# A two-layer block on eight cores: second-layer chunks one step later, and the front of the next token tile behind the statistics

## The reference

```
xn   = layernorm(x) * gamma + beta
v, g1, g2 = split(xn @ W_in + b_in)            # 1024 -> 3 x 1024
y    = conv(conv(v, k0) * g1, k1) * g2         # causal, 128 taps, per channel
x    = layernorm(x + (x + y @ W_out + b_out))
# feed-forward with quantized activations and ternary weights
bitlinear(x, nw, w) = quant(rmsnorm(x) * nw) @ ternary(w).T   # quant: round(x * 127 / max|x|) / scale
h    = act_scale * relu(bitlinear(x, norm1_w, w1))**2 + act_bias   # 1024 -> 4096
out  = layernorm(x + bitlinear(h, norm2_w, w2))                    # 4096 -> 1024
```

## Time and profile before

| | us |
|---|---|
| median of 3 runs | 3107.97 (3107.31 to 3112.25) |
| the profiled execution | 3111.75 |
| its span, slowest core (core 4) | 3110.2 |
| spans of the 8 cores | 3085.6 to 3110.2 |
| busy: TensorE / weight load / VectorE / ScalarE / GpSimd | 1383.4 / 430.3 / 1522.5 / 786.9 / 72.7 |
| DMA queue of SyncE (q1) | 186716 packets, 82.34 MB |

### The profile page before, as it was taken

The page is one execution under the profiler, slowest core; times in us unless marked ns, Lnnn a source line. Parts: engine busy times, 40 slices in busy tenths (PEclk is TensorE's granted clock), DMA queues, the critical chain, the costliest instruction groups (busy, mean ns, idle before and its releaser), DMA issues.

```text
span 3110.2 us, 19372 instructions; the slowest of 8 cores (3085.6 to 3110.2 us)
## 1 busy us (share of the span) xinstructions
PE 1383.4 (44%) x4270; PEld 430.3 (14%) x4270; DVE 1522.5 (49%) x1611; ACT 786.9 (25%) x1164; POOL 72.7 (2%) x128
## 2 busy tenths in 40 slices
PE   0666566676666610000023554444554443455453
PEld 0122122222212100000001111111111111111110
DVE  2223434334343434555124566655566665566665
ACT  0010111111111000000004444444444444444442
POOL 0000000000000011101000000000000000000000
PEclk9888777777877755555556666666766666676775
DMA  3410000000000035668830100100110010011011
GB/s 87 142 34 0 11 21 11 11 21 11 21 11 14 7 124 174 208 253 277 195 73 13 27 17 24 24 24 23 26 28 16 23 24 24 23 27 28 15 23 27
DMA packets 203436, 166.43 MB, mean 54 GB/s; under 512 B 173625, under 2 KB 178490, under 8 KB 199227
## 3 DMA queue, kind: packets, MB, share of 16 engines
q1 hardware_dynamic: 186716, 82.34, 10.4%
q0 software_dynamic: 16608, 82.85, 8.5%
HBM read 100.09 MB, written 29.36 MB: 42 GB/s over the span
## 4 chain that ended last, share of the span: by engine, by line
DVE 35%; issue 14%; PEldq 13%; DMA 13%; SPq 9%; ACT 9%; PEld 4%; DVEq 2%; ACTq 1%; POOLq 0%
PEldq L175 13%; DVE g2s L882 8%; DMA wqf<-w 8%; SPq L1014 6%; DVE Pb L656 5%; ACT d2s L875 2%; DVE xq2o L888 2%; DVE f2s L872 2%; DMA xq2Tc<-xq2o 2%; DMA xp<-sc_xp 2%; SPq L837 1%; DVE wqb L804 1%; DVE d2s L885 1%; DVE st_mu L510 1%; SPq L830 1%
## 5 line engine op out<-in xcount | busy, mean ns | idle before, releaser
L1023 PE MATMUL yc<-wq2T,xq2Tc 128*128 128x512 bf16 x1024 | 380.7, 492 | 678.7 <-DMA xq2Tc<-xq2o 666.1
L882 DVE SCALAR_TENSOR_TENSOR g2s<-d2s,g2s 128x1024 bf16<-128x1024 bf16 x288 | 352.9, 1225 | 35.2 <-issue 1.3
L984 PE MATMUL pj<-wq1T,xq1T 128*128 128x512 bf16 x1024 | 305.2, 433 | 120.6 <-DMA xq1T<-xq 84.3
L1023 PEld LDWEIGHTS yc<-wq2T,xq2Tc 128*128 128x128 bf16 x1024 | 110.5, 112 | 941.9 <-issue 911.4
L934 ACT ACTIVATE t<-xp 128x1024 f32<-128x1024 bf16 x16 | 16.9, 1056 | 554.2 <-PEq L175 481.8
L1043 DVE TENSOR_TENSOR t2f<-t2f,nw2r 128x1024 f32<-128x1024 f32 x64 | 78.4, 1225 | 148.8 <-ACTq L175 141.4
L875 ACT ACTIVATE d2s<-f2s 128x1024 bf16<-128x1024 bf16 x64 | 67.6, 1056 | 321.1 <-DVEq L175 321.1
L984 PEld LDWEIGHTS pj<-wq1T,xq1T 128*128 128x128 bf16 x1024 | 99.4, 105 | 334.1 <-issue 270.9
L598 PE MATMUL pj<-Wg,xnT 128*128 128x512 bf16 x288 | 110.6, 553 | 73.1 <-DVEq L175 73.1
L598 PE MATMUL yc<-Wg,xnT 128*128 128x512 bf16 x576 | 136.7, 380 | 2.9
L665 PE MATMUL pj<-Pb,s_winv 128*128 128x512 bf16 x198 | 98.4, 566 | 84.6 <-DVEq L175 84.6
(11 more groups left out here) (181 smaller groups left out, 2054.6 us busy)
## 6 DMA issues: line engine op xcount, KB each, us to landing
wqf<-w POOLq DMA_DIRECT2D x64, 512.0 KB, 4.3
wqf<-w POOLq DMA_DIRECT2D x16, 2048.0 KB, 12.0
wf<-W_in SPq DMA_DIRECT2D x8, 1536.0 KB, 7.1
xr<-x_own POOLq DMA_DIRECT2D x16, 512.0 KB, 4.0
sc_wq<-wqb SPq DMA_DIRECT2D x32, 256.0 KB, 2.4
sc_wq<-wqb SPq DMA_DIRECT2D x8, 1024.0 KB, 5.2
xq2Tc<-xq2o SPq DMA_TRANSPOSE x512, 2.3
out<-outb SPq DMA_DIRECT2D x16, 512.0 KB, 2.9
```

Source lines behind the costliest of these rows:

```text
L882: tn = sch.op("vector", (lambda lv: lambda e: e.scalar_tensor_tensor(gbuf[:, 0:width], dbuf[:, 0:width], 0.5 + lv, gbuf[:, 0:width], OP.is ...
L984: (lambda ss, dc, h: lambda e: e.matmul(pshalf("pj", h), xq1T[:, dc * 128:(dc + 1) * 128], wq1T[dc][:, ss * 1024 + h * 512: ss * 1024 + (h ...
L1023: (lambda k, q, oc, kb: lambda e: e.matmul(pshalf("yc1", oc), xq2Tc[kb][:, q * 128:(q + 1) * 128], wq2Tc[k * 8 + q][:, oc * 512:(oc + 1) * ...
```

## The change

Two things are reordered in stage 3, and nothing else changes.

First, the loop over `k` in a pass runs six steps instead of five, and T chunk `k-2` is emitted in step `k` where it was T chunk `k-1`. The SV chunks and superstrips keep their steps.

Second, F of tile `t+1` is emitted after the statistics of tile `t`, where it stood at the start of the pass; the eight transposes of `xq1` belong to it again and are no longer a function of their own. F is thus followed by the final add of tile `t-1`.

```diff
@@ emit_stageF
         free["t1"] = tq1
-        d["tq1"] = tq1
-        return d
-
-    def emit_xq1T(d):
-        tq1 = d["tq1"]
         trq1 = []
         for c in range(8):
             trq1.append(sch.op("sync", (lambda c: lambda e: e.dma_start(
...
         free["xq1"] = tuple(trq1)
+        return d
@@ the loop over t
         if t == 0:
             Fst[0] = emit_stageF(0)
-            emit_xq1T(Fst[0])
-        if t + 1 < NT:
-            Fst[t + 1] = emit_stageF(t + 1)
         tok_sc = [None] * 4
         tq2s = {}
         tmm2_last = None
-        for k in range(5):
+        for k in range(6):
             if t >= 1 and k < 4:
                 tq2s[k] = emit_chunkSV(t - 1, k)
             if t < NT and 1 <= k <= 4:
                 th2_tok = emit_superstrip(t, k - 1)
                 tok_sc[k - 1] = emit_stat_chunk(t, k - 1, th2_tok)
-            if t >= 1 and k >= 1:
-                tmm2_last = emit_chunkT(t - 1, k - 1, tq2s[k - 1])
-        if t + 1 < NT:
-            emit_xq1T(Fst[t + 1])
+            if t >= 1 and k >= 2:
+                tmm2_last = emit_chunkT(t - 1, k - 2, tq2s[k - 2])
         if t < NT:
             Sst[t] = emit_stats(t, tok_sc)
+        if t + 1 < NT:
+            Fst[t + 1] = emit_stageF(t + 1)
```

## The result

The changed kernel takes 3022.5 us (median of 8 runs, 3020.4 to 3023.6); the kernel before 3108.4 in the same comparison. The ratio is 0.9721 with a 95% interval of 0.9711 to 0.9732: 2.8% faster, 85.9 us. Forecast were 3029.2 and a range of 3011 to 3060. The profiled execution's span is 3021.8 us on core 5 (3110.2 on core 4 before).

A forecast was written before the change was run, and what follows sets the result against it. No engine is full; the stage is a chain with holes, VectorE standing in it most often. 13 x 5.87 = 76.3, + 11.9 - 11.8 + 2.4 = 78.8 us off 3111.75: 3033.0, on the median 3029.2; range 3011 to 3060.

The forecast's parts named there:

- F: Front stage of a tile (L938 to L888 on xq1), forecast to take 14.37 us.
- E3: Moment VectorE ends a tile's fourth SV chunk; E3 to SV0 forecast at 37.37 us against 43.24.
- SV0: First L872 on f2s of the next pass, forecast 8.03 us behind the end of F.
- The wait before stat 3: VectorE's hole before stat 3: superstrip 3 behind T chunk 1 brings it to E3 + 3.9 to 5.6, from 11.6.
- stat 3: The fourth L1043 of a tile on VectorE, forecast at E3 + 3.9 to 5.6.
- The load as the new last wait: Load of xp on SyncE behind T chunk 3's transposes: issued E3 + 10.60, 4.37 us later F starts, E3 + 14.97.
- The tail: After F: final add, sums, normalization, then SV0, 8.03 us with 3.19 idle for the cast F used to cover.
- The ends: First and last tiles of the stage: gain 11.9 us at the start, loss 11.8 at tile 13, gain 2.4 at tile 14.
- stat 3 stays late: Rival: superstrip 3 meets another wait, F starts at E3 + 18.8, 50 us of gain go: 3079; chance 0.06.
- the load takes all the gain: Rival: load of xp reaches VectorE 10.2 us after issue, E3 to SV0 stays 43.2: 3108; chance 0.02.
- superstrip 0 becomes the bound: Rival: next tile's F, transposes and matmuls in series delay Relu 0; slower, 3138 if 31 us; chance 0.04.
- the fourth rival: Transposes issued so fast VectorE never waits for the load; F at about E3 + 11: 2973; chance 0.04.

The follow-up runs named there:

- Experiment 7: Changed kernel with the load of xp ahead of T chunk 0, SV0's cast ahead of the final normalization, and two superstrip accumulators: 2906.8 us, ratio 0.9350.
- Experiment 5: Changed kernel with the load of xp for the next tile issued ahead of T chunk 0, not behind T chunk 3: 2983.7 us, ratio 0.9597.
- experiment 6: Changed kernel with the load of xp ahead of T chunk 0 and the next SV0's cast ahead of the final normalization: 2934.8 us, ratio 0.9436.
- experiment 2: Changed kernel with T chunks back at k-1 in five steps, F still behind the statistics: 3068.0 us, ratio 0.9872 to the kernel before.
- experiment 4: Changed kernel with the eight transposes of xq1 put behind the store of out on SyncE: 3022.5 us, ratio 0.9733 to the kernel before.

## Why the prediction was right, point by point

**In short.** Each wait went and came where the prediction has it, and the median was 6.7 us under the forecast. That the gain a tile came out so close is partly luck: both terms of the difference were too long, and the errors partly cancel. From E3 to SV0 the tile of the earlier trace rows takes 43.24 us, but the thirteen tiles of before take 42.6 on average; afterwards it is 36.3 where 37.37 was forecast. So 0.6 us too much before and 1.1 us too much after left 5.87 forecast against 6.3. Outside E3 to SV0 a tile changed by 0.1 us, which makes up the measured 6.45.

**The wait before stat 3.** Right in its cause. The prediction put stat 3 at E3 + 3.9 to 5.6. It came at 4.7 to 6.1, on average at 5.3; at 5.78 in the tile above, because superstrip 3 ran slow:

```profile
2410.68 6.19 PE L980 MATMUL pj<-wq1T,xq1T 128*128 128x512 bf16 x16 [6.24 <-ACTq L175]
2417.09 3.61 PE L1019 MATMUL yc<-wq2T,xq2Tc 128*128 128x512 bf16 x16 [0.23 <-issue]
```

After 6.24 us of idleness its sixteen matmuls took 6.19 us, at a mean granted clock of 0.60 (1 is full speed, 2.4 GHz; the lower level is 0.5, 1.2 GHz); those of T chunk 2 right behind it took 3.61, at 1.00. So superstrip 3 ran mostly at the lower level after the pause, and the clock was back at the upper one by T chunk 2. The slow value of the earlier trace rows, 6.07, has a clock of 0.61, and the 4.41 one of 0.87; the slower one was nearer. It cost nothing here, since the load was later still. Experiment 7 shows what it is worth once the load is out of the way.

**The load as the new last wait.** Right. F was forecast at E3 + 14.97 and came at 14.82 (14.6 on average): issue 0.17 later than forecast, load to F 4.05 where the earlier trace rows have 4.37. Experiment 5 shows it as the bound. The Trainium skill (Advanced Engine Details and Errata, section X-Bar Transpose (TRN2)) says that transposing DMAs are as fast as regular ones on this chip. The trace does not bear that out for transposes of 32 KB: eight held SyncE for 10.48 us here too, and one load of 256 KB for 0.52. Experiment 5, which moves the load ahead of all 32 transposes of the T chunks, is worth 39 us.

**The tail.** The wait of 3.13 before SV0 is the cast, as forecast (3.19); experiment 6 took it away.

**The mis-sized term: F.** It was given 14.37 us, from one tile, and takes 13.71. Part of this was a choice of row: in that tile VectorE had one stall of 0.54 us before L885, 0.35 above the usual. The other 0.38 was not foreseen. (In most tiles of before F takes 14.0 us, not 14.37.) ScalarE's cast in F, first before and then after:

```profile
2515.60 0.20 ACT L912 ACTIVATE st_tmpb<-st_tmpb 128x1 f32<-128x1 f32 x1
2516.59 1.15 ACT L869 ACTIVATE it2s<-t,st_m 128x1024 int32<-128x1024 f32 x1 [0.79 <-DVEq L175]
```

```profile
2434.63 0.20 ACT L912 ACTIVATE st_tmpb<-st_tmpb 128x1 f32<-128x1 f32 x1
2435.24 1.15 ACT L869 ACTIVATE it2s<-t,st_m 128x1024 int32<-128x1024 f32 x1 [0.41 <-DVEq L175]
```

With the new order the cast waits for one semaphore instead of eight: by the time F comes, ScalarE has already waited for later values of the seven DMA lanes. F's share of the 1.1 us that the forecast had too much in each tile is 0.66; the other 0.4 is F's earlier start. The stretch from SV0 to E3, which the prediction left alone, takes 48.8 us, and took 48.9 before.

**The ends.** Tile 0's SV0 was forecast at 1689.9 and came at 1686.43. Half of that is the superstrips of tile 0, which follow each other in 5.25 us each, where the earlier trace rows have one of 6.96; the rest is F's start (0.65), F itself (0.35) and stat 0 (0.7). In the forecast's own terms the spans give 15.35 us at the start (11.9 forecast), 83.2 in thirteen tiles (76.3), a loss of 10.95 at tile 13 (11.8), 1.4 at tile 14 (75.09 to 73.71, where 2.4 was forecast) and a loss of 0.6 behind it (nothing): 88.4, where 78.8 were forecast. The median moved by 2.5 us less than the span of the profiled executions, whose slowest cores are not the same.

**The rivals.** That stat 3 stays late is what experiment 2 is, and it cost 46 us against the changed kernel, where 50 were worked out for it. That the load takes all the gain, and that superstrip 0 becomes the bound, were tested in experiments 5 and 4 and don't hold. More gain was there to be had by moving the load; no run made the transposes faster, which is what the fourth rival was about, and SyncE's rows speak against it.

## What to carry to other kernels

When no engine is full, follow one tile from a fixed event and write down, for each in-order queue, what stands ahead of the late instruction; a hole can have another right behind it, and is then worth only the distance between the two. Take a term from several tiles, not from one. Two reorderings can be worth more together than apart: one frees the early instruction, the other puts other work ahead of what is now last. A load that needs no result should not stand in a queue behind DMAs that wait for one, and a cast or other small step whose cover is moved away should move with it.

## What the runs showed of the hardware that was not expected

- An instruction's list of waits has a price, even when all of them have long been reached. By the code, ScalarE's cast in F has eight semaphores to wait for in tiles 1 to 15 of before and one in tile 0. ScalarE idles 0.79 us ahead of it in fourteen of these fifteen tiles (1.07 in the other), and 0.41 in tile 0. In the changed kernel it has eight in F(1) only, which shows 0.79, and one in all others, which show 0.41:

```profile
1677.02 1.15 ACT L869 ACTIVATE it2s<-t,st_m 128x1024 int32<-128x1024 f32 x1 [0.79 <-DVEq L175]
```

- That is 0.38 us for seven more waits, some 54 ns each by this estimate. SV0's cast in the changed kernel, which now waits for seven lanes, bears it out: it starts 0.49 us behind the instruction ahead of it. SV1's waits for none and starts 0.10 us behind. So what F saves is paid again before SV0; the forecast had that in its 8.03 us, a row in which this cast waits for eight. No run changed the number of waits and nothing else.
- TensorE's superstrips became slower while the kernel became faster: 522 ns a matmul in the mean, 433 before, while the T chunks went from 492 to 426. It is the clock: between 1700 and 2960 us the mean granted clock while superstrips ran fell from 0.83 to 0.62, and while T chunks ran it rose from 0.69 to 0.87. From the first final add on, TensorE stood idle for 3 to 16 us ahead of each superstrip of the changed kernel, and for 0.2 to 0.3 us before.

```profile
L980 PE MATMUL pj<-wq1T,xq1T 128*128 128x512 bf16 x1024 | 388.6, 522 | 592.4 <-DMA xq1T<-xq 332.7
L1019 PE MATMUL yc<-wq2T,xq2Tc 128*128 128x512 bf16 x1024 | 291.9, 426 | 124.0 <-DMA xq2Tc<-xq2o 107.5
```
